# Where the first operands of a fused conv and quantized FFN are issued: ScalarE's queue or SyncE's

## The chip, the core and the metric

The kernel runs on one core of a Trainium2 chip. The metric is the device time of one execution in microseconds; below 291.45 us is the median of three executions. Lower is better.

## What is computed

`x` is 128 x 32 x 512 (tokens x channels x length), f32. A grouped 1-d convolution over the length (4 groups of 8 channels, 9 taps) is shifted by a conditional term, and the result goes through a feed-forward block whose activations and weights are all rounded to 8-bit steps; `x` is added at the end:

```python
out = conv(x, weight, groups=4, padding=4)            # 128 x 32 x 512
out = out + (c @ c_weight.T)[:, :, None] + bias[None, :, None]
gate = qlinear(out, w_gate)                           # 512 -> 1376
up   = qlinear(out, w_up)                             # 512 -> 1376
y = x + qlinear(silu(gate) * up, w_down)              # 1376 -> 512
# qlinear(x, w): x and w rounded by fake_quant to steps of max|row| / 127, then multiplied
```

## The kernel before

The convolution is done on TensorE: `x_windows` holds the input cut in 32 **spans** (4 groups g of 8 spans i, each 320 KB, 64 positions of 8 channels), and `toeplitz_cut[:, g]` holds the taps of group g spread as a **band** (80 KB for one group). `conv_span(q)` makes five windows of span q, each one f32 product that TensorE runs as two passes, so ten matmuls a span. It waits for the span (`span_in[q]`) and, at the first span of a group, for that group's band (`taps_in` for group 0). The small operands, `small_sb` (96 KB: the condition, its weight and the bias), give the per-channel shift: `multiply_ctx` on TensorE waits for `small_in`, `make_shift` on VectorE waits for it too, and every `add_shift` waits for `shift_ready`.

The weights `w_gate_up` come in 11 tiles of 512 KB (`load_w(j)`), the down weights in 4 pieces of 688 KB (`load_w_down(o)`). VectorE takes their row maxima (`weights_top`, `down_top`), GpSimd rounds them (`round_w`), TensorE turns them (`turn_gate_up`), ScalarE copies them out. Once the weights are in place, 32 channels run as tiles i = 0 to 31: gate and up products in three pieces (`gate_or_up`), silu, scaling, a maximum over the row, rounding, a DMA transpose, and the down product (`down`).

Each engine runs a fixed list of steps, written out by hand for the first part and as a loop from tile 7 on; nothing is moved at run time. What orders the start:

- **SyncE's queue** issues nearly all DMAs. It begins with `load_span(0)`, `load_span(1)`, `load_w(0)`, `load_span(2)`, `load_span(3)`, `load_span(4)`, `load_w(1)` and goes on alternating spans and weights. Its first wait is in `load_w(10)`, for the turn of weight tile 0 (`w_turned`, L311), and `load_w_down(0)` to `(2)` follow behind that.
- **ScalarE's queue** issues two DMAs at its start (L609, L610): the band of group 0 and the small operands. Then ScalarE waits for the small operands and runs one `Silu` on a column of them (L612, L613, the "silu trial", whose result nothing reads, so that the table of the activation is loaded early). Then come `copy_span(2)` and the rest.
- **VectorE** clears `warm_in` (L916, counted by `warm_ready`), then `weights_top(0)`, `make_shift`, `add_shift(0)`, `add_shift(1)`, `fold_y(1)`.
- **TensorE** waits for `warm_ready`, runs seven matmuls on the cleared tile (`run_empty(7)`), waits for the identity matrices, and goes through `conv_span(0)`, `conv_span(1)`, `multiply_ctx()`, `conv_span(2)` to `conv_span(8)`, `turn_gate_up(0)`, `conv_span(9)`, `conv_span(10)` and the turns of the weights.

Of the kernel before, what the change touches and what calls it, by code (L numbers as in the profile page):

```python
# [6 lines left out]
ACT = mybir.ActivationFunctionType  # L7
# [20 lines left out]
def adaln_ffn(nc, x, x_windows, cond_ctx_bias, taps_cut, w_gate_up, w_down, out):  # L28
    N, C, L = x.shape
    BLOCK = 4 * PAD  # L30
    CI = P // BLOCK
# [19 lines left out]
    CUT_WIDTH = LEAST + 2 * SHARED  # L51
# [16 lines left out]
    with ExitStack() as ctx:  # L68
        def sb(name, shape, dt=F32):
            return ctx.enter_context(nc.sbuf_tensor(name, shape, dt))  # L70

        def sem(name):
            return ctx.enter_context(nc.semaphore(name))
# [15 lines left out]
        toeplitz_cut = sb("toeplitz_cut", [P, GROUPS, CI, CUT_WIDTH])  # L89
        ident = sb("ident", [P, P])  # L90
        ident_bf = sb("ident_bf", [P, P], BF16)
        small_sb = sb("small_sb", [P, N + 2 * C])
        silu_trial = sb("silu_trial", [P, 1])
        warm_in = sb("warm_in", [P, P], BF16)
# [18 lines left out]
        def span_windows(g, i):  # L113
            return slabs[g % 2][:, WINDOWS * i:WINDOWS * (i + 1), :]
# [63 lines left out]
        small_in = sem("small_in")  # L178
        taps_in = sem("taps_in")
# [5 lines left out]
        warm_ready = sem("warm_ready")  # L185
# [104 lines left out]
        def rows(j):  # L290
            return P if j < JT - 1 else TAIL
# [4 lines left out]
        def _(sp):  # L296
            def load_span(q):
                g, i = divmod(q, SPANS)
                if i == 0 and g == 2:

                    sp.wait_ge(wdq_ready, KT - 1)
                elif i == 0 and g == 3:

                    sp.wait_ge(conv_done, 2 * SPANS)
                sp.dma_start(span_windows(g, i).rearrange("p w n -> p (w n)"), x_windows[g, :, i, :])\
                    .then_inc(span_in[q], 16)

            def load_w(j):
                if j >= W_SLOTS:

                    sp.wait_ge(w_turned, j - W_SLOTS + 1)  # L311
                r = rows(j)
                sp.dma_start(w_in[j % W_SLOTS][0:r, :, :], w_gate_up[P * j:P * j + r, :, :])\
                    .then_inc(w_tile_in[j % W_SLOTS], 16)
# [68 lines left out]
            def load_other_taps():  # L383
                sp.dma_start(toeplitz_cut[:, 2:, :, :].rearrange("p g c o -> p (g c o)"), taps_cut[:, 2 * CI * CUT_WIDTH:])\
                    .then_inc(taps_cut_in, 16)

            load_span(0)
            load_span(1)
            load_w(0)
            load_span(2)  # L390
            load_span(3)
# [214 lines left out]

        @block.scalar
        def _(act):
            act.dma_start(toeplitz_cut[:, 0, :, :].rearrange("p c o -> p (c o)"), taps_cut[:, 0:CI * CUT_WIDTH]).then_inc(taps_in, 16)  # L609
            act.dma_start(small_sb[:, :], cond_ctx_bias).then_inc(small_in, 16)  # L610

            act.wait_ge(small_in, 16)  # L612
            act.activation(silu_trial[:, :], small_sb[:, 0:1], ACT.Silu)  # L613

            def copy_span(q):
                g, i = divmod(q, SPANS)
# [776 lines left out]
```

## Time and profile before

| | us |
|---|---|
| median of three executions | 291.45 |
| fastest of the three / slowest of the three | 290.97 / 757.24 |
| the profiled execution, its own time | 292.09 |
| its span, first to last instruction | 290.3 |
| outside the span | 1.8 |
| TensorE busy / VectorE busy in the span | 279.6 / 250.0 |
| TensorE's granted clock over the span | 1.00 |

In the rows further down, PE is TensorE, PEld its weight loads, DVE VectorE, ACT ScalarE, POOL GpSimd, SPq and ACTq the issuing of SyncE and ScalarE; L305 is line 305 of the kernel. A DMA row tells how long the issue held the queue, and "to landing" is the time from the start of the issue to the completion that a waiting engine sees. Buffer numbers and tile shares of one memory are left out in names: `hq_mem<-w_gate_up` is one of the first six weight tiles, `slab<-x_windows` a span, `slab<-w_down` one of the first three down pieces.

### The profile page before, as it was taken

Reading aid. Unit: us, or ns where it says so; the run is one execution under the profiler, and the core shown is the slowest. Engines: PE = TensorE matmul, PEld = TensorE weight load, DVE = VectorE, ACT = ScalarE, POOL = GpSimd, SP = SyncE. Lnnn points to the kernel's source line nnn. Section 1 sums busy time; section 2 is a strip of 40 time slices with the busy share of each in tenths; the row PEclk is TensorE's granted clock in tenths of the full one; section 3 lists DMA queues with packets and bytes.
Section 4 is the critical chain, followed back from the end, with each engine's and each line's share of the span. In section 5 each row is a group of like instructions: output and inputs, shape, how many; then the busy total and the mean of one; then the engine's idle time right before and its main releaser. Section 6 shows DMA issues by size and latency. Waiting matters only on the chain.

```text
span 290.3 us, 4758 instructions
## 1 busy us (share of the span) xinstructions
PE 279.6 (96%) x1582; PEld 160.0 (55%) x1582; DVE 250.0 (86%) x410; ACT 193.8 (67%) x232; POOL 200.9 (69%) x209
## 2 busy tenths in 40 slices
PE   7897989999999999999999999999989999999995
PEld 4896656656455555554444656664434444444443
DVE  0998999899998998979888888898978889888885
ACT  2349989898687776555877744555688767666640
POOL 1469988999858786555788834556488887666623
PEclk9999999999999999999999999999999999999999
DMA  7999943594929999853599995523266683333346
GB/s 254 412 416 345 395 150 76 133 223 94 264 80 233 242 218 223 176 163 99 129 232 275 294 216 166 161 78 96 75 158 159 169 198 87 87 88 86 97 99 209
DMA packets 83848, 53.37 MB, mean 184 GB/s; under 512 B 69904, under 2 KB 70672, under 8 KB 83696
## 3 DMA queue, kind: packets, MB, share of 16 engines
q1 hardware_dynamic: 83536, 52.89, 66.8%
q8 instruction: 13, 0.21, 0.3%
q10 hardware_dynamic: 288, 0.18, 0.2%
q14 instruction: 11, 0.09, 0.1%
HBM read 27.75 MB, written 8.39 MB: 125 GB/s over the span
## 4 chain that ended last, share of the span: by engine, by line
PE 78%; DMA 8%; DVE 5%; POOL 4%; issue 3%; SPq 0%; ACT 0%; DVEq 0%; POOLq 0%
PE bank L1201 45%; PE bank L1221 20%; PE bank L1103 12%; DMA slab<-w_down 6%; DMA slab<-x_windows 2%; POOL sg_mem L519 2%; DVE h_mem L879 1%; DVE h_max L884 1%; DVE sg_mem L866 1%; POOL slab L527 1%; DVE hq_mem L905 1%; POOL xo_mem L527 0%; POOL yq_mem L500 0%; DVE y_part L844 0%; POOL y_mem L510 0%
## 5 line engine op out<-in xcount | busy, mean ns | idle before, releaser
L1201 PE MATMUL bank<-wgu_t,xq_mem 128*128 128x512 bf16 (+1 forms) x768 | 155.8, 357 | 2.6 <-DVE sg_mem L866 1.3
L519 POOL TENSOR_TENSOR sg_mem<-sg_mem,gu_scale_row 128x512 f32<-128x512 f32 (+1 forms) x96 | 111.2, 1165 | 60.7 <-ACT sg_mem L665 60.6
L1201 PEld LDWEIGHTS bank<-wgu_t,xq_mem 128*128 128x128 bf16 x768 | 73.8, 98 | 74.2 <-DVE h_mem L879 7.9
L665 ACT ACTIVATE sg_mem<-sg_mem,x_scale 128x512 f32<-128x512 f32 (+1 forms) x96 | 62.7, 672 | 38.9 <-DVE sg_mem L866 38.7
L1221 PE MATMUL bank<-wd_t,hq_mem 128*128 128x512 bf16 (+1 forms) x341 | 78.6, 379 | 0.1
L879 DVE SCALAR_TENSOR_TENSOR h_mem<-bank,x_scale,sg_mem 128x512 f32<-128x512 f32 (+1 forms) x96 | 65.8, 690 | 11.1 <-POOL sg_mem L519 9.2
L866 DVE TENSOR_TENSOR sg_mem<-bank,gu_scale_row 128x512 f32<-128x512 f32 (+1 forms) x96 | 59.8, 626 | 13.7 <-PE bank L1201 13.6
L670 ACT ACTIVATE h_mem<-h_mem,h_inv 128x1376 f32<-128x1376 f32 (+1 forms) x32 | 45.1, 1414 | 25.5 <-DVE h_inv L786 25.5
L1221 PEld LDWEIGHTS bank<-wd_t,hq_mem 128*128 128x128 bf16 (+1 forms) x341 | 33.3, 98 | 40.4 <-DMA hq_mem<-hq_mem 0.6
L884 DVE TENSOR_REDUCE h_max<-h_mem 128x1 f32<-128x1376 f32 x32 | 50.3, 1575 | 0.0
L1103 PEld LDWEIGHTS bank<-toeplitz_cut,slab 128*128 128x128 f32 x320 | 43.0, 191 | 4.5 <-issue 1.3
L1103 PE MATMUL bank<-toeplitz_cut,slab 128*128 128x160 f32 (+1 forms) x320 | 43.8, 290 | 1.4 <-DMA slab<-x_windows 0.8
L678 ACT ACTIVATE hq_mem<-h_mem 128x1376 bf16<-128x1376 f32 (+1 forms) x32 | 41.8, 1310 | 0.1
L527 POOL TENSOR_TENSOR xo_mem<-xo_mem,hq_mem 128x512 f32<-128x512 f32 x24 | 30.5, 1273 | 1.9 <-DMA xo_mem<-x 1.9
L905 DVE SCALAR_TENSOR_TENSOR hq_mem<-bank,h_scale,wd_scale_row 128x512 f32<-128x512 f32 x31 | 23.0, 743 | 1.5 <-POOL slab L527 1.3
L629 ACT ACTIVATE y_mem<-y_mem,x_inv 128x512 f32<-128x512 f32 x24 | 16.1, 710 | 2.1 <-DVE x_inv L786 2.1
L500 POOL TENSOR_SCALAR yq_mem<-y_mem 128x512 bf16<-128x512 f32 x22 | 13.3, 619 | 3.0 <-ACT y_mem L629 3.0
L844 DVE TENSOR_REDUCE y_part<-y_mem 128x8 f32<-128x1024 f32 x12 | 14.6, 1214 | 0.2
L793 DVE TENSOR_REDUCE gu_max<-hq_mem 128x2 f32<-128x1024 f32 (+1 forms) x7 | 8.3, 1198 | 6.6 <-DMA hq_mem<-w_gate_up 6.6
L510 POOL TENSOR_TENSOR y_mem<-y_mem,shift 128x512 f32<-128x512 f32 x7 | 7.3, 1050 | 9.3 <-ACT y_mem L622 9.3
L483 POOL TENSOR_SCALAR hq_mem<-hq_mem,gu_inv 128x512 f32<-128x512 f32 (+1 forms) x14 | 9.5, 693 | 3.2 <-DVE gu_inv L805 3.2
L641 ACT ACTIVATE wgu_t<-bank 128x1024 bf16<-128x1024 int16 (+1 forms) x11 | 10.9, 1034 | 0.4 <-PE bank L1119 0.4
(63 smaller groups left out, 136.4 us busy)
## 6 DMA issues: line engine op xcount, KB each, us to landing
slab<-x_windows SPq DMA_DIRECT2D x32, 320.0 KB, 4.1
xo_mem<-x SPq DMA_DIRECT2D x24, 256.0 KB, 2.9
out<-xo_mem SPq DMA_DIRECT2D x24, 256.0 KB, 2.2
hq_mem<-w_gate_up SPq DMA_DIRECT2D x6, 512.0 KB, 8.9
slab<-w_down SPq DMA_DIRECT2D x3, 688.0 KB, 15.0
h_mem<-w_gate_up SPq DMA_DIRECT2D x4, 512.0 KB, 13.5
slab<-x SPq DMA_DIRECT2D x1, 2048.0 KB, 9.7
out<-slab SPq DMA_DIRECT2D x7, 256.0 KB, 2.0
```

The costliest lines, as they stand in the source:

```text
L519: pool.tensor_tensor(s, s, gu_scale_row[:, 1, at:at + n], ALU.mult).then_inc(silu_scaled, 1)
L527: pool.tensor_tensor(xo_of(i), xo_of(i), down_out[:, i % 2, :], ALU.add).then_inc(out_ready, 1)
L665: act.activation(s, s, ACT.Silu, scale=x_scale[:, i:i + 1]).then_inc(silu_done, 1)
L670: act.activation(hi, hi, ACT.Copy, bias=MAGIC, scale=h_inv[:, i:i + 1]).then_inc(h_rounded, 1)
L678: act.activation(hq[i % HQ_BUFS][:, first:INTER], h[i % H_BUFS][:, first:], ACT.Copy, bias=-MAGIC)\
L866: dve.tensor_tensor(sg[i % SG_BUFS][:, at:at + n], gate_bank[(NP * i + p) % 2][:, 0:n], gu_scale_row[:, 0, at:at + n], ALU.mult).then_inc( ...
L879: dve.scalar_tensor_tensor(h[i % H_BUFS][:, at:at + n], up_bank[(NP * i + p) % 2][:, 0:n], x_scale[:, i:i + 1], sg[i % SG_BUFS][:, at:at + ...
L884: dve.tensor_reduce(h_max[:, i:i + 1], h[i % H_BUFS], AX_X, ALU.max, apply_absolute_value=True)\
L905: dve.scalar_tensor_tensor(down_out[:, i % 2, :], down_bank_of(i)[:, :], h_scale[:, i:i + 1], wd_scale_row[:, :], ALU.mult, ALU.mult).then ...
L1103: last = pe.matmul(out_span[:, :, lo:hi], span_windows(g, i)[:, k, :], toeplitz_cut[:, g, :, tap:tap + hi - lo], start=(k == 0), stop=(k = ...
L1201: last = pe.matmul(bank[n % 2][:, 0:cols], xq_t[:, g, k, P * c:P * (c + 1)], wgu_t[:, m, k, at:at + cols], start=(k == 0), stop=(k == KT - 1))
L1221: last = pe.matmul(down_bank_of(i)[:, :], hq_t[i % HQT_BUFS][0:r, j, :], wd_t[0:r, j, :], start=(j == 0), stop=(j == JT - 1))
```

## The change

The two DMAs of ScalarE's queue go to SyncE's: the band of group 0 becomes its very first DMA, ahead of span 0, and the small operands its fourth, behind span 1 and ahead of weight tile 0. The silu trial no longer waits for the small operands and reads them; it waits for the cleared tile `warm_in` and reads a column of that. Nothing else differs: the same bytes are moved, and every consumer waits on the same semaphores.

```diff
@@ SyncE
+            sp.dma_start(toeplitz_cut[:, 0, :, :].rearrange("p c o -> p (c o)"), taps_cut[:, 0:CI * CUT_WIDTH]).then_inc(taps_in, 16)
             load_span(0)
             load_span(1)
+            sp.dma_start(small_sb[:, :], cond_ctx_bias).then_inc(small_in, 16)
             load_w(0)
             load_span(2)
             load_span(3)
@@ ScalarE
-            act.dma_start(toeplitz_cut[:, 0, :, :].rearrange("p c o -> p (c o)"), taps_cut[:, 0:CI * CUT_WIDTH]).then_inc(taps_in, 16)
-            act.dma_start(small_sb[:, :], cond_ctx_bias).then_inc(small_in, 16)
-
-            act.wait_ge(small_in, 16)
-            act.activation(silu_trial[:, :], small_sb[:, 0:1], ACT.Silu)
+
+            act.wait_ge(warm_ready, 1)
+            act.activation(silu_trial[:, :], warm_in[:, 0:1], ACT.Silu)
```

## Rows read from the trace of the kernel before

**Rows 1.** Busy time by stretch: us, PE, PEld, DVE, ACT, POOL, clock, DMA share, GB/s.

```profile
0.00:10.00 10.00, 7.58 (x42) 5.38 (x43) 2.58 (x5) 1.61 (x3) 1.21 (x10) 1.00 0.82 297
...
40.00:280.00 240.00, 238.78 (x1263) 128.73 (x1262) 212.91 (x353) 169.51 (x197) 172.13 (x165) 1.00 0.64 158
```

**Rows 2.** Waits of TensorE, whole span: line, waited for, us in total, times, longest.

```profile
PE bank L1119 <- POOL hq_mem L483: 1.5, 3, 0.7
PE bank L1201 <- DVE sg_mem L866: 1.3, 1, 1.3
PE bank L1103 <- DMA slab<-x_windows: 0.8, 1, 0.8
PE bank L1103 <- DMA toeplitz_cut<-taps_cut: 0.6, 1, 0.6
```

**Rows 3.** The chain that ended last, in order of time, first 39 us: start, us.

```profile
1.66 0.42 SPq L313
2.08 0.04 issue
2.12 6.16 DMA slab<-x_windows
8.28 0.04 issue
8.33 9.29 PE bank L1103 x70
...
20.74 16.16 DMA slab<-w_down
```

**Rows 4.** Timeline of TensorE, 0 to 17 us: start, us, instruction, idle before.

```profile
4.60 2.75 PE L1103 MATMUL bank<-toeplitz_cut,slab 128*128 128x112 f32 x20 [0.61 <-DMA toeplitz_cut<-taps_cut]
7.19 0.32 PE L1175 MATMUL bank<-small_sb 128*128 128x32 f32 x2
8.33 9.29 PE L1103 MATMUL bank<-toeplitz_cut,slab 128*128 128x112 f32 x70 [0.82 <-DMA slab<-x_windows]
```

**Rows 5.** One issue a query: taps, then small operands, span 0, weight tile 0.

```profile
L609 ACTq DMA_DIRECT2D toeplitz_cut<-taps_cut x1: 407/407/407, 0.7 to 0.7; - x1
DMA to landing us min/median/max: 3.7/3.7/3.7
...
DMA to landing us min/median/max: 4.2/4.2/4.2
...
DMA to landing us min/median/max: 3.5/3.5/3.5
...
DMA to landing us min/median/max: 5.8/5.8/5.8
```

**Rows 6.** Timeline of SyncE's queue, 0 to 21 us.

```profile
0.74 0.87 SPq L305 DMA_DIRECT2D slab<-x_windows  x2
...
12.64 1.43 SPq L313 DMA_DIRECT2D h_mem<-w_gate_up  x2
18.09 0.34 SPq L313 DMA_DIRECT2D hq_mem<-w_gate_up  x1
```

**Rows 7.** Busy time from the start to six moments; last column GB/s over it.

```profile
0.00:2.00 2.00, 1.01 (x3) 0.43 (x4) 0.11 (x1) 0.33 (x1) 1.21 (x10) 1.00 0.15 22
0.00:2.50 2.50, 1.51 (x4) 0.58 (x5) 0.11 (x1) 0.83 (x1) 1.21 (x10) 1.00 0.27 45
0.00:3.50 3.50, 2.51 (x6) 0.89 (x7) 0.11 (x1) 1.28 (x1) 1.21 (x10) 1.00 0.46 121
0.00:4.50 4.50, 3.00 (x7) 0.89 (x7) 0.11 (x1) 1.28 (x1) 1.21 (x10) 1.00 0.58 178
0.00:6.00 6.00, 4.40 (x18) 2.31 (x19) 0.11 (x1) 1.49 (x2) 1.21 (x10) 1.00 0.68 226
3.00:37.00 34.00, 30.32 (x269) 26.15 (x268) 27.58 (x42) 20.50 (x30) 21.80 (x29) 1.00 1.02 385
```

**Rows 8.** Timeline of ScalarE, 0 to 10 us.

```profile
1.67 1.28 ACT L613 ACT_TABLE_LOAD   x1 [1.67 <-PEq L1387]
5.45 0.20 ACT L613 ACTIVATE silu_trial<-small_sb 128x1 f32<-128x1 f32 x1 [2.50 <-DMA small_sb<-cond_ctx_bias]
9.88 0.60 ACT L622 ACTIVATE y_mem<-bank 128x512 f32<-128x512 f32 x1 [4.22 <-PE bank L1103]
```

**Rows 9.** Timeline of VectorE, 7 to 38 us.

```profile
7.50 1.22 DVE L793 TENSOR_REDUCE gu_max<-hq_mem 128x2 f32<-128x1024 f32 x1 [6.57 <-DMA hq_mem<-w_gate_up]
8.63 0.18 DVE L821 TENSOR_TENSOR shift<-bank,small_sb 128x32 f32<-128x32 f32 x1
...
36.92 1.58 DVE L809 TENSOR_REDUCE d_max<-slab 128x1 f32<-128x1376 f32 x1 [0.37 <-DMA slab<-w_down]
```

## Prediction

> **What bounds the kernel now.** I read the busy time by stretches first. From 40 to 280 us TensorE works for 238.78 of 240 us at a granted clock of 1.00 [rows 1]; nothing that is issued in the first 15 us can shorten that, so the change can only be worth what it alters at the start. There TensorE is busy 7.58 of the first 10 us [rows 1], and the table of its waits says what for: 0.6 us for the band of group 0 and 0.8 us for a span near the beginning, then 1.5 us behind GpSimd's rounding and 1.3 us behind VectorE later [rows 2]. The 0.6 us is the wait that the change aims at. Whether it counts is told by the timeline: the first two spans run from 4.60 to about 7.3, the small product to 7.51, and then TensorE idles 0.82 us more, until span 2 has landed [rows 4]. So two waits stand in a row, and the second ends last. An earlier start of the first span only makes the second wait longer, as long as span 2 lands where it does now. The chain of waits agrees: it doesn't pass through the band, it passes through the landing of span 2 at 8.28, 70 matmuls, and then the landing of the third down piece at 36.90 [rows 3].
>
> The third thing to read is what those landings hang on. From 3 to 37 us the DMA engines are busy at a share of 1.02, moving 385 GB/s [rows 7]. Span 2 is issued at 2.12 and lands 6.16 us later, the down piece 16.16 us after its chain step [rows 3], while span 0 needed 3.5 us [rows 5]: these transfers stand in line behind the bytes ahead of them. In this stretch the time is set by the sum of bytes, and only where the line runs dry by the moment of issue.
>
> **The change, part by part.**
>
> *The small waits on ScalarE.* Removed: two issues on ScalarE's queue, of 0.41 us for the band, and the wait of the trial. The table load starts at 1.67, behind the issues, and the trial runs at 5.45 after 2.50 us of waiting; then ScalarE idles 4.22 us until the first span that it copies [rows 8]. After, the table load can start near 0.8 and the trial near 2.1. That is worth 0: the next work of ScalarE waits for TensorE, not for the trial. The cover is those 4.22 us, and the new wait is for a memset of VectorE that TensorE's warm-up waits for as well. If that cover were gone, the trial would cost its 0.20 us.
>
> *The band goes first on SyncE.* It saves nothing in bytes and delays span 0 by one issue. Two issues hold the queue for 0.87 us in all [rows 6], so one step is some 0.45 us. Now the band lands at 0.74 + 3.7 = 4.5 and span 0 at 0.74 + 3.5 = 4.2, and the first matmul starts at 4.60 [rows 4, 5]. After, the start hangs on span 0. Lower bound: the two shared the engines, and their sum of bytes is served by the same moment as now, so span 0 lands at about 4.2, and TensorE starts 0.3 us earlier. Upper bound: the landing moves by the whole step, 4.2 + 0.45 = 4.7, and TensorE starts at 4.75, 0.15 us later than now. Even then the first two spans and the small product, 2.9 us as they run now (4.60 to 7.51 [rows 4]), end at 7.66, ahead of 8.28. Worth to the end: 0 on both bounds, with 0.6 us of cover.
>
> *The small operands behind span 1.* Issued at about 2.1 rather than 1.18. They landed 4.2 us after their issue, at 5.4 [rows 5]. A shift of the full 0.9 us gives 6.3; the small product is not reached before 7.1, and the shift is made at 8.63, behind the maximum of weight tile 0 [rows 4, 9]. Cost 0, cover 0.8 us.
>
> *What is queued behind them.* Every later DMA of SyncE is issued later, weight tile 0 and span 2 by two steps, 0.9 us. This is the only part that can reach the end, so it is worked through with bytes. From the start of the first issue (0.74) to the first data is about 1 us: 44 KB have moved by 2.0 [rows 7]. In units of 1000 bytes the new line is: band 82, span 0 328, span 1 328, small 98, weight tile 0 524, then span 2. What was moved by a moment is the mean rate by the length: 112 by 2.5, 424 by 3.5, 801 by 4.5, 1356 by 6.0 [rows 7]. So the engines reach the bytes of
>
> - span 0 (82 ahead) at 2.2; it is available at 1.19 + 1.0 = 2.2: just in time
> - span 1 (410 ahead) at 3.5; available at 2.6
> - small operands (738 ahead) at 4.3; available at 3.1
> - weight tile 0 (836 ahead) at 4.6; available at 3.5
> - span 2 (1360 ahead) at 6.0; available at 4.0
>
> Only at span 0 can the line run dry, and by no more than one step, 0.45 us. Behind it the margin is 0.9 us and grows. Later, SyncE ends its run of issues at 14.07 and stands until 18.09 for the turn of weight tile 0 [rows 6]; 0.9 us more of issuing falls into those 4.0 us. If that cover were gone, the remaining weight tile and the down pieces would be issued up to 0.9 us later, and they stand in line for over 12 us anyway.
>
> So the shift of the DMA stream, call it d, has bounds of nothing lost and 0.45 us lost, and below nothing too: the order by which two queues shared the engines in the first 5 us is gone, and the third down piece is waited for by VectorE with 0.37 us of idle time [rows 9], so at most 0.37 us could be gained before VectorE's own work ends last. I take d = +0.1: the arithmetic says that the line is just supplied, and the packets that meet the slow first microsecond are now the band's small ones, so a few bytes less get through in it. From the down piece d goes on to the end in full, since VectorE's next steps release TensorE (the 1.3 us wait [rows 2]) and TensorE has no slack after 40 us.
>
> The Trainium skill ("DMA: Bandwidth & Descriptors", section "Issuing engines are not separate DMA queues") says that all issuing engines use the same 16 DMA engines, and that issuing from several only saves the sequencer's issue time. That speaks against this change, since it gives up exactly that saving: by the rule alone, with the issue time taken as it stands, the sum would be two steps worse, which is the first rival below; by the rows the saving is hidden behind the line.
>
> **Sum.** Start of the first span -0.3 to +0.15, worth 0; trial 0; small operands 0; stream +0.1 (-0.37 to +0.45). The profiled execution, 290.3 in its span and 1.8 around it, becomes 290.4 and 292.2. That execution stands 0.6 us above the median of the runs, so against the median of 291.45 the forecast is 291.55; I give 291.5.
>
> **Rivals.**
>
> *A, slower: the issue time goes through.* The chain runs over the issues ahead of span 2 (L313 ends at 2.08, span 2 is issued at 2.12 [rows 3]). If landings follow the issue and not the line, weight tile 0 and span 2 come 0.9 us later: span 2 at 9.2, VectorE's first maximum at 8.4 instead of 7.50 [rows 9], and everything that was DMA-bound or VectorE-bound moves with them: 291.45 + 0.9 = 292.35. It decides from the point where d exceeds 0. For it: the chain as printed. Against it: 6.16 us from issue to landing where 3.5 is possible, and a share of 1.02. A chance of 0.13.
>
> *B, faster: the start is gained.* The band no longer trickles in between the packets of spans 0 and 1, the stream starts with small packets in the slow first microsecond and runs at its full rate sooner, and span 2, weight tile 0 and the down piece all land earlier. Price: up to the 0.37 us of VectorE's idle time before the third down piece: 291.45 - 0.37 = 291.1. It decides if span 2 lands before 8.1. Against it: the bytes are the same. A chance of 0.20.
>
> *C, the fixed order falls into another step.* A shift of some tenths lets the loop meet another wait, such as the one of 1.1 us on VectorE that the busy shares show as 238.78 of 240 [rows 1]. All waits of TensorE named in rows 2 sum to 4.2 us, so doubling one of them costs some 1.5 us (292.95), losing one gains as much (289.95). A chance of 0.07.
>
> The forecast itself holds 0.60. Its own range is the spread of executions, which for the kernel before goes from 290.97 to 292.09, shifted by 0.1. The range down to B's gain and up to A's cost on the same spread is 290.97 - 0.37 = 290.6, and 292.09 + 0.9 = 293.0; I give 290.5 to 292.9.
>
> Two per cent, about what a measurement of this kernel can tell from no change, is 5.8 us. No case comes near: A and B stay within it, and C would need several waits at once. I leave 0.01 for faster and 0.02 for slower, 0.97 for within.
>
> **What would show it.** Right, if in the changed kernel TensorE's first span starts between 4.2 and 4.8, waits for `slab<-x_windows` and no longer for the band, if span 2 still lands at 8.2 to 8.5 with TensorE's second wait as long as the first start allows, if weight tile 0 is seen by VectorE at 7.4 to 7.7, if the third down piece lands at 36.7 to 37.2, and if the trial runs near 2.1 with ScalarE's next copy still near 9.9. If span 2 lands at 9.2, A holds; if the DMA stream ends before 36.6, B. The forecast is wrong if the stream's share between 2 and 3 us drops by more than 0.45 us of work, or if an engine past 40 us shows a wait that isn't there now.

## The result and the profile after

The changed kernel is slower: a median of 293.64 us against 291.80 us for the kernel before, 16 executions of each. The ratio of the fast executions, which leaves out the one of 757.24 us, is 1.0054 with a 95% interval of 1.0034 to 1.0074, so 1.6 us, from 1.0 to 2.2. That is within the 2% of the forecast's main case, but outside its range of 290.5 to 292.9. The profiled execution took 293.72 us with a span of 291.9, against 292.09 and 290.3.

The chain of waits of the changed kernel, in order of time, from the fourth issue on (start, us, what):

```profile
2.11 0.43 SPq L390
2.54 0.04 issue
2.59 0.43 SPq L313
3.02 0.04 issue
3.06 5.96 DMA slab<-x_windows
9.03 0.04 issue
9.07 9.32 PE bank L1103 x70
...
21.50 16.00 DMA slab<-w_down
```

Against [rows 3], span 2 is issued at 3.06 rather than 2.12, and it lands at 9.02 rather than 8.28. The two added issues moved it by 0.94, and 0.74 of that arrived. The third down piece lands at 37.50 rather than 36.90. The chain still doesn't pass through the band.

TensorE's timeline and ScalarE's, of the changed kernel:

```profile
4.59 3.92 PE L1103 MATMUL bank<-toeplitz_cut,slab 128*128 128x112 f32 x20 [0.43 <-issue]
8.35 0.32 PE L1175 MATMUL bank<-small_sb 128*128 128x32 f32 x2
...
2.02 0.20 ACT L613 ACTIVATE silu_trial<-warm_in 128x1 f32<-128x1 bf16 x1
10.62 0.60 ACT L622 ACTIVATE y_mem<-bank 128x512 f32<-128x512 f32 x1 [8.39 <-PE bank L1103]
```

The first span starts at 4.59, as before (4.60 [rows 4]); nothing was gained there even locally. But the 20 matmuls of the first two spans now take 3.92 us, until 8.5, rather than 2.75. That isn't the change's doing, and it is no wait: a matmul takes some 480 ns up to 6.5 us, where it takes some 290 ns in the kernel before, and the granted clock stands at 1.00 in both. The kernel before has it too, in a second profile of the unchanged text (taken further down), first TensorE's timeline and then the chain of waits:

```profile
4.71 5.22 PE L1103 MATMUL bank<-toeplitz_cut,slab 128*128 128x112 f32 x20 [0.55 <-DMA toeplitz_cut<-taps_cut]
...
0.73 3.84 DMA toeplitz_cut<-taps_cut
4.57 0.14 issue
4.71 5.22 PE bank L1103 x20
```

Over the twenty profiles the same 20 matmuls take from 2.75 to 5.22 us; why isn't shown. The trial runs at 2.02 without a wait and gives nothing, since ScalarE's next copy waits for TensorE until 10.62; it stood at 9.88 [rows 8].

Where the DMA engines lost the time is told by the busy time from 4 to 8 us (us, PE, PEld, DVE, ACT, POOL, clock, DMA share, GB/s). Before, and then after:

```profile
4.00:8.00 4.00, 2.90 (x22) 2.82 (x22) 0.50 (x1) 0.20 (x1) 0.00 (x0) 1.00 1.01 389
```

```profile
4.00:8.00 4.00, 3.57 (x18) 3.44 (x18) 0.00 (x0) 0.00 (x0) 0.00 (x0) 1.00 0.90 306
```

83 GB/s less over 4 us are 332 KB, which take 0.85 us at the 389 GB/s of the kernel before. This stretch, in which the forecast had the engines well supplied, holds most of what the start lost.

Where the start's loss has arrived at TensorE is best read at its first eight gate and up products in one run, just behind the down pieces (before, then after):

```profile
39.16 1.90 PE L1201 MATMUL bank<-wgu_t,xq_mem 128*128 128x512 bf16 x8 [1.34 <-DVE sg_mem L866]
```

```profile
39.77 1.90 PE L1201 MATMUL bank<-wgu_t,xq_mem 128*128 128x512 bf16 x8 [1.00 <-DVE sg_mem L866]
```

They are 0.61 us later. In the profiles of all experiments this row starts at 38.47 to 39.50 us in the eight that issue their DMAs up to 7 us as the kernel before does, and at 39.59 to 40.09 in the five that do it as the changed one does; the means are 0.7 us apart.

The other place is at 81 us, at GpSimd's first residual add (before, then after):

```profile
81.00 2.52 POOL L527 TENSOR_TENSOR xo_mem<-xo_mem,hq_mem 128x512 f32<-128x512 f32 x2 [1.92 <-DMA xo_mem<-x]
```

```profile
82.33 2.50 POOL L529 TENSOR_TENSOR xo_mem<-xo_mem,hq_mem 128x512 f32<-128x512 f32 x2 [2.64 <-DMA xo_mem<-x]
```

GpSimd was free for it at 81.00 - 1.92 = 79.08 and at 82.33 - 2.64 = 79.69: the start's 0.61 us. Then it waited 0.72 us longer for residual 0, and from there to the end both stay in the distance (1.3 us, and 0.3 more at the end, where the changed kernel's TensorE waits 0.5 us for a turn). In sixteen of the eighteen profiles that issue residual 0 in its place, the span is the start of this add and 209.2 to 209.8 us; so what two profiles differ by is nearly all made ahead of it. So one profile has two parts, and the experiments take them in turn.

### The profile page after: what moved, and what is told of

It reads as the page before. It is cut to its first block, busy times and chain, and to the rows that moved or that the text cites. A ratio compares the mean times of both kernels' runs of the same rounds, so it can differ in the third digit from the quotient of the medians.

```text
span 291.9 us, 4758 instructions
## 1 busy us (share of the span) xinstructions
PE 281.1 (96%) x1582; PEld 161.2 (55%) x1582; DVE 249.4 (85%) x410; ACT 193.8 (66%) x232; POOL 200.8 (69%) x209
## 4 chain that ended last, share of the span: by engine, by line
PE 70%; DMA 11%; DVE 5%; issue 4%; POOL 4%; ACT 3%; SPq 2%; DVEq 0%; POOLq 0%; ACTq 0%
PE bank L1201 41%; PE bank L1221 17%; PE bank L1103 11%; DMA slab<-w_down 5%; POOL sg_mem L521 2%; DMA slab<-x_windows 2%; DMA xo_mem<-x 2%; ACT h_mem L670 1%; DMA hq_mem<-hq_mem 1%; DVE h_mem L879 1%; DVE h_max L884 1%; ACT hq_mem L678 1%; POOL xo_mem L529 1%; DVE sg_mem L866 1%; POOL yq_mem L502 1%
## 5 line engine op out<-in xcount | busy, mean ns | idle before, releaser
L1103 PEld LDWEIGHTS bank<-toeplitz_cut,slab 128*128 128x128 f32 x320 | 44.2, 195 | 4.8 <-DMA slab<-x_windows 1.4
L1103 PE MATMUL bank<-toeplitz_cut,slab 128*128 128x160 f32 (+1 forms) x320 | 45.0, 295 | 1.3 <-DMA slab<-x_windows 0.9
L622 ACT ACTIVATE y_mem<-bank 128x512 f32<-128x512 f32 x7 | 4.2, 594 | 11.8 <-PE bank L1103 11.8
```

Source lines behind the costliest of these rows:

```text
L1103: last = pe.matmul(out_span[:, :, lo:hi], span_windows(g, i)[:, k, :], toeplitz_cut[:, g, :, tap:tap + hi - lo], start=(k == 0), stop=(k = ...
```

## Experiments

Theory I: what counts is the issue step, a DMA put ahead of weight tile 0 and span 2 on SyncE's queue. Rivals: S, the sharing of the engines by two queues; the trial; and G, later C, for the second part.

| kernel | median us | before beside it | ratio, 95% |
|---|---|---|---|
| band alone | 292.87 | 292.19 | 1.0016, 0.9995 to 1.0037 |
| small operands alone | 293.00 | 292.19 | 1.0027, 1.0010 to 1.0045 |
| trial alone | 292.28 | 292.19 | 0.9998, 0.9982 to 1.0014 |
| the change again | 293.90 | 292.19 | 1.0062, 1.0040 to 1.0084 |
| two useless DMAs, early | 293.56 | 291.70 | 1.0061, 1.0039 to 1.0082 |
| weight tile 0 by ScalarE | 291.73 | 291.70 | 1.0003, 0.9981 to 1.0025 |
| residual 0 earlier, before | 292.04 | 291.70 | 1.0010, 0.9996 to 1.0025 |
| residual 0 earlier, changed | 293.63 | 291.70 | 1.0055, 1.0033 to 1.0077 |
| four useless DMAs, early | 293.82 | 291.89 | 1.0076, 1.0042 to 1.0109 |
| two useless DMAs, at 7 us | 292.99 | 291.89 | 1.0034, 1.0012 to 1.0057 |
| span 1 by ScalarE | 292.44 | 291.89 | 1.0019, 1.0001 to 1.0037 |
| spans 3 and 4 in one DMA | 293.09 | 291.89 | 1.0038, 1.0016 to 1.0061 |
| ten small matmuls, before | 292.41 | 292.53 | 0.9998, 0.9979 to 1.0017 |
| ten small matmuls, changed | 293.28 | 292.53 | 1.0023, 1.0005 to 1.0041 |
| six warm-ups fewer | 294.87 | 292.53 | 1.0073, 1.0042 to 1.0103 |
| thirty small matmuls | 292.65 | 292.23 | 1.0007, 0.9987 to 1.0026 |

### The parts of the change, one by one

```diff
 # band alone: SyncE
+            sp.dma_start(toeplitz_cut[:, 0, ...], taps_cut[:, 0:CI * CUT_WIDTH]).then_inc(taps_in, 16)
             load_span(0)
             load_span(1)
 # small operands alone: SyncE
+            sp.dma_start(small_sb[:, :], cond_ctx_bias).then_inc(small_in, 16)
             load_w(0)
 # trial alone: ScalarE
+            act.wait_ge(warm_ready, 1)
+            act.activation(silu_trial[:, :], warm_in[:, 0:1], ACT.Silu)
```

> Only the band of group 0 goes to SyncE's queue, first; the small operands and the trial stay as before. Theory I (issue steps: each DMA put ahead of weight tile 0 and span 2 on SyncE's queue moves their landings by nearly its 0.45 us, and so the end): span 2 lands near 8.65, half of the change's loss, +0.6 to +0.9 us. Theory S (sharing: what is lost is the sharing of the engines by two queues in the first microseconds, since the band alone leaves the engines empty from 2.5 to 3 us): nearly the whole loss, +1.3 to +1.6 us, with the DMA share of 2.5 to 3.0 us at about 0.6 as in the changed kernel.

> Only the small operands go to SyncE's queue, behind span 1; the band stays first on ScalarE's. Theory I (issue steps): weight tile 0 and span 2 one step later, span 2 at 8.65, +0.6 to +0.9 us. Theory S (sharing in the first microseconds): nothing is empty between 2.5 and 3 us, span 2 stays near 8.3, 0 to +0.2 us.

> Only the silu trial's wait and input are changed; both DMAs stay on ScalarE's queue. Theories I and S: no difference (-0.2 to +0.2 us), the table load still starts at 1.67 behind the two issues. A theory that the trial matters would have +0.5 us or more.

> The changed kernel once more, as the measure for the three others on the same chip: +1.3 to +1.9 us, and a second profile of it. Theory I: span 2 lands at 9.0 again. If the landing of span 2 differs by 0.5 us or more between the two profiles while the time doesn't, the start isn't what the loss hangs on.

Measured: +0.7 for the band (its interval reaches just below nothing), +0.8 for the small operands, +0.1 for the trial, and +1.7 for all. The parts add up within their intervals, and both issues are near the half that theory I gave them. The trial is out. S had expected next to nothing of the small operands, 0 to +0.2; their interval, from 0.3 us on, excludes that. It had also expected a DMA share of 0.6 from 2.5 to 3.0 us with the band alone; that was 1.08. Nor did span 2 land at 8.65: with the band alone it landed at 9.08, and with the small operands alone TensorE began it at 8.45. From 4 to 8 us the engines moved 295 GB/s with the band alone and 350 with the small operands alone:

```profile
4.00:8.00 4.00, 3.73 (x23) 3.60 (x22) 0.00 (x0) 0.00 (x0) 0.00 (x0) 1.00 0.90 295
```

```profile
4.00:8.00 4.00, 2.93 (x23) 2.82 (x22) 0.33 (x1) 0.20 (x1) 0.00 (x0) 1.00 0.95 350
```

### Issue steps without bytes

```diff
+            sp.dma_start(tiny[:, 0:2], cond_ctx_bias[:, 0:2]).then_inc(tiny_in, 16)
             load_span(0)
             load_span(1)
+            sp.dma_start(tiny[:, 2:4], cond_ctx_bias[:, 2:4]).then_inc(tiny_in, 16)
             load_w(0)
```

> The kernel before, with both operands still on ScalarE's queue, and two DMAs of 8 bytes a partition added to SyncE's at the two places where the change puts its own (ahead of span 0, behind span 1). They are work of no use; the output is as before. Theory I (issue steps: weight tile 0 and span 2 land later because they are issued two steps later): nearly the full loss of the change, +1.2 to +1.8 us, VectorE's first maximum at 8.0 or later. Theory S (the loss is that the band and the small operands leave ScalarE's queue, so that one queue alone must keep the engines busy): 0 to +0.3 us, the maximum at 7.5.

Measured: +1.9 us, the whole loss, with ScalarE's queue as it was and 1 KB in each added DMA. VectorE's first maximum and the stretch from 4 to 8 us of this kernel:

```profile
8.78 1.22 DVE L798 TENSOR_REDUCE gu_max<-hq_mem 128x2 f32<-128x1024 f32 x1 [7.85 <-DMA hq_mem<-w_gate_up]
...
4.00:8.00 4.00, 3.16 (x14) 3.04 (x13) 0.00 (x0) 0.20 (x1) 0.00 (x0) 1.00 0.85 294
```

The maximum comes at 8.78, where it was 7.50 [rows 9], and the rate is lower than the changed kernel's 306. S falls; it is the steps on SyncE's queue.

Do twice as many cost twice as much, and does it matter where they stand?

```diff
 # four: two ahead of span 0, two behind span 1
 # late: one ahead of and one behind load_taps_of_group_1()
             load_span(8)
+            sp.dma_start(tiny[:, 0:2], cond_ctx_bias[:, 0:2]).then_inc(tiny_in, 16)
             load_taps_of_group_1()
+            sp.dma_start(tiny[:, 2:4], cond_ctx_bias[:, 2:4]).then_inc(tiny_in, 16)
             load_w(3)
```

> The kernel before with four useless DMAs of 8 bytes a partition on SyncE's queue, two ahead of span 0 and two behind span 1. Theory I (each early issue step costs): two steps cost 1.9 us, so four cost 3.4 to 4.2 us, and the engines move some 220 GB/s or less between 4 and 8 us (389 before, 294 with two). A theory that the loss comes from the first step that uncovers the engines and then saturates: 1.7 to 2.4 us.

> The kernel before with the two useless DMAs placed later on SyncE's queue, around the load of the band of group 1 at 7.2 us. Theory L (only steps issued before the line of transfers has built up count, since later ones lie behind 8 us of queued bytes): 0 to +0.3 us. A theory that every issue on SyncE's queue costs, because the queue itself is the bound all the way: +1.5 us or more.

Both missed. Four steps cost +1.9 in the median, with an interval of 1.2 to 3.2 us: that excludes the 3.4 and more of theory I, but not that four cost more than two. In their profiles they do, with the eight products at 41.05 against 40.43; from 4 to 8 us the engines moved 323 GB/s. Late steps leave the start as it is in the profile (394 GB/s from 4 to 8 us, the eight products at 39.15), and yet the median is +1.1 with an interval from 0.4 to 1.7. So two added DMAs can cost as much as that without touching the start, and a part of what the early ones cost need not be made there either. Something differs between executions that a single profile doesn't catch.

### Fewer steps than before

```diff
 # weight tile 0 by ScalarE's queue, behind the small operands
-            load_w(0)
+            act.dma_start(w_in[0][0:P, :, :], w_gate_up[0:P, :, :]).then_inc(w_tile_in[0], 16)
 # span 1 by ScalarE's queue, between the band and the small operands
-            load_span(1)
+            act.dma_start(span_windows(0, 1)..., x_windows[0, :, 1, :]).then_inc(span_in[1], 16)
 # spans 3 and 4 in one DMA; conv_span(3) waits for span_in[4]
-            load_span(3)
-            load_span(4)
+            sp.dma_start(slabs[0][:, WINDOWS * 3:WINDOWS * 5, :]..., x_windows[0, :, 3:5, :]...).then_inc(span_in[4], 16)
```

> The opposite of the change: weight tile 0 goes from SyncE's queue to ScalarE's, behind the small operands, so that span 2 and all later DMAs of SyncE are issued one step earlier. Theory I: span 2 lands at 7.9 rather than 8.3 and the end moves by -0.3 to -0.8 us. Theory S or a stream bound by its bytes alone: 0 within 0.2 us. A rival: tile 0 shares the engines with spans 2 to 4 and VectorE's first maximum comes later than 7.5, then +0.2 to +0.6 us.

> Span 1 goes from SyncE's queue to ScalarE's, between the band and the small operands, so that weight tile 0, span 2 and all later DMAs of SyncE are issued one step earlier and weight tile 0 isn't held back on a shared queue. Theory I with steps that still cost in the kernel before: -0.3 to -0.8 us. If the kernel before is already supplied from 4 to 8 us (389 GB/s of the 415 that the engines reach later), nothing is left to gain: -0.2 to +0.2 us.

> Spans 3 and 4 of the kernel before are loaded by one DMA of 640 KB, so that weight tile 1 and everything behind it are issued one step earlier; the price is that span 3 is only seen when span 4 has landed too, at about 9.9 rather than 9.1, and TensorE reaches span 3 at 9.6. Theory I (steps cost): the gain of a step, up to -0.4, against 0.3 us of waiting for span 4, so -0.1 to +0.3. If steps behind span 2 don't count: +0.2 to +0.4.

None gained. With tile 0 on ScalarE's queue span 2 was issued at 1.68 but landed at 9.10, not at the 7.9 of theory I, and tile 0 itself reached VectorE at 8.93; yet the rate is 394 GB/s and the median that of the kernel before. So a late span 2 alone doesn't cost; the versions that lose at the start are those with a lower rate from 4 to 8 us. With span 1 on that queue, +0.5. The merged load is the instructive one. Its start is the best of all:

```profile
4.00:8.00 4.00, 3.62 (x26) 3.49 (x26) 1.36 (x2) 0.20 (x1) 0.00 (x0) 1.00 1.05 421
```

and its first residual add is

```profile
81.98 2.49 POOL L527 TENSOR_TENSOR xo_mem<-xo_mem,hq_mem 128x512 f32<-128x512 f32 x2 [3.91 <-DMA xo_mem<-x]
```

GpSimd was free at 78.07, 1.0 us ahead of the kernel before, and waited 3.91 us in place of 1.92. In this profile the gain of the start was given back twice over, and the median was +1.2.

### Is it the gate at 81 us?

```diff
             turn_hq(3)
+            load_residual(0)
             load_span(18)
             load_span(19)
-            load_residual(0)
```

> The kernel before, with the load of residual 0 issued ahead of spans 18 and 19 rather than behind them (near 76 us). In the profiles GpSimd's first residual add waits for it at 81 us and everything behind it moves by what it is late. Theory G (the gate at 81 us takes a part of the change's loss): here it is worth 0 to -0.8 us, as the gate is sometimes closed in this kernel too. A theory in which all of the loss is made in the first 40 us: 0 within 0.2.

> The changed kernel with the same move of residual 0. Theory G: of the loss of 1.7 us against the kernel before, only the part made in the first 40 us is left, 0.6 to 1.0 us, and the step at 81 us is gone from the profile. A theory in which all of the loss is made in the first 40 us: still +1.5 to +1.9 us.

Theory G gets no support: with residual 0 issued ahead of the two spans the medians are still 1.6 us apart, and neither is faster. It isn't excluded, since the two ratios differ by 0.0045 with an uncertainty of 0.0026, so by 0.5 to 2.1 us, and G had 0.6 to 1.0. In the profile of the kernel before the first add then came at 78.89, but the second waited 2.38 us for VectorE:

```profile
78.89 1.27 POOL L527 TENSOR_TENSOR xo_mem<-xo_mem,hq_mem 128x512 f32<-128x512 f32 x1 [0.29 <-DMA xo_mem<-x]
82.53 1.27 POOL L527 TENSOR_TENSOR xo_mem<-xo_mem,hq_mem 128x512 f32<-128x512 f32 x1 [2.38 <-DVE hq_mem L905]
```

The place is a gate, but opening it alone only hands the wait on.

### What holds the residual up: a load of the instruction queue

In the profile with the merged load, residuals 1 and 2, issued at about 72 us, take 6 us to land, and the turn behind them 6.9; in the kernel before it is 3.3 and 4.2. Between them a packet of 16 KB stands on the queue called "instruction" (q8). There are 13 of them in the page for 1582 matmuls, one to 122. Theory C: that load, falling among the transposes and residuals, is slow and holds them up. The unchanged kernel was profiled a second time for it:

> The kernel before once more, as it is, for a second profile of it: all theories have the third down piece at 36.4 to 37.0 us and 388 to 396 GB/s between 4 and 8 us. Theory C: if the load on the instruction queue stands ahead of 72 us and takes about 1 us there is no step at 81 us, and if it takes over 2 us there is one of 1.4 to 2.0 us.

Its span was 292.0 and its time 293.79, with nothing changed. The DMA queues in the microsecond of the load, first of the profile that the prediction rests on (70 to 71 us), then of this one (74 to 75 us):

```profile
q8 instruction: 1, 0.02, 6.0%
```

```profile
q8 instruction: 1, 0.02, 15.7%
```

6.0% of 16 engines for 1 us is 0.96 us for the one packet, and 15.7% is 2.5 us. And this profile's issues of the two residuals, its queue and its add:

```profile
L341 SPq DMA_DIRECT2D xo_mem<-x x2: 413/468/524, 72.9 to 73.5; - x2
DMA to landing us min/median/max: 5.6/5.6/5.7
...
73.95 3.41 SPq L352 DMA_TRANSPOSE hq_mem<-hq_mem  x1
77.41 1.05 SPq L305 DMA_DIRECT2D slab<-x_windows  x2
78.56 0.38 SPq L341 DMA_DIRECT2D xo_mem<-x  x1
...
82.83 2.49 POOL L527 TENSOR_TENSOR xo_mem<-xo_mem,hq_mem 128x512 f32<-128x512 f32 x2 [3.52 <-DMA xo_mem<-x]
```

The turn's issue holds the queue 3.41 us (2.28 before), residual 0 is issued 1.4 us later, and the add waits 3.52, 1.6 us more, as theory C had it for a load of over 2 us. All profiles with residual 0 in its place, by their load (its share times 16 us) and the add's wait:

| load near 64 to 79 us | profiles | wait of the add, us |
|---|---|---|
| 64 to 72 us, 1.0 to 1.5 us long | before; trial; change again; change, third profile; two early; two late; ten matmuls, changed; six fewer; thirty | 1.92; 1.57; 1.95; 1.86; 1.57; 1.62; 1.52; 1.76; 1.12 |
| 77 to 79 us, 1.0 to 1.2 us long | change; small operands; tile 0 by ScalarE | 2.64; 2.95; 2.51 |
| 73 to 76 us, 1.9 to 3.1 us long | before, second profile; band; span 1 by ScalarE; merged; four early; ten matmuls, before | 3.52; 3.33; 3.74; 3.91; 3.90; 2.94 |

The first group stands apart from the other two (at most 1.95 against at least 2.51); the second and the third touch (2.95 and 2.94). The same kernel stands in the first and the third (the kernel before), and in the first and the second (the changed one). So the wait goes with when the load falls, and that isn't fixed by the kernel's text. Which of the two sets the other is open. In ten profiles the load ahead of this one stands at 44 to 49 us and the one behind it at 94 to 96 (85 with the thirty matmuls below), but this one between 64 and 78, and at 69, 70 and 78 in the three of the changed kernel: it may be late and long because the transfers around it are, and not the other way round. That was tried by moving the load:

```diff
 # ten, in the kernel before and in the changed one
             run_empty(7)
+            for _ in range(10):
+                pe.matmul(conv_bank(3)[:, 0:32], warm_in[:, :], warm_in[:, 0:32], start=True, stop=True)
 # six warm-ups fewer
-            run_empty(7)
+            run_empty(1)
 # thirty: run_empty(4) and the loop over range(30)
```

> The kernel before with ten more matmuls of 32 columns on the cleared tile behind run_empty (work of no use, in time in which TensorE waits for the band anyway), so that TensorE's program is 20 instructions longer ahead of everything. Theory C (a 16 KB load on the instruction queue, one to about 125 of TensorE's matmuls, falls near 70 to 78 us; where it falls among the DMA transposes and residual loads issued at 71 to 75 us it takes 2.5 us rather than 1.0, holds them up and costs 1.4 to 2.0 us at GpSimd's first residual add): the load comes 2 us earlier, clear of them, -0.2 to -0.8 us in the median and no step at 81 us in the profile. Rival R (the step at 81 us has nothing to do with that load): 0 within 0.2 us, steps as often as before.

> The changed kernel with the same ten matmuls. Theory C: no step at 81 us either, so that against the same edit of the kernel before only the part made in the first 40 us is left, +0.7 to +1.1 us. Rival R: still +1.6 to +1.9 us apart.

> The kernel before with run_empty(1) in place of run_empty(7): TensorE's program is 12 instructions shorter ahead of everything (six warm-up matmuls are left out, their result is not used). Theory C: the load on the instruction queue comes about 1.3 us later, at 71 to 73 us, among the transposes and residual loads more often: +0.5 to +1.5 us, with a load of over 2 us and a step of 1.4 to 2.0 us at 81 us in the profile. Rival R: 0 within 0.2 us, unless TensorE's granted clock falls, which the profile would show.

In the kernel before, the ten matmuls did not clear the place: the load stands at 73 us with 1.9 us, within the 70 and 74 of that kernel's own two profiles, the add waits 2.94, and the median doesn't move. In the changed kernel the load went to 68 us, the add waits only 1.52, and the medians of the two are 0.87 us apart, as theory C had it. The two ratios (0.9998 and 1.0023) differ by 0.0025 with an uncertainty about as large, so this doesn't separate 0.9 from 1.6 us for certain.

Six warm-ups fewer missed its place (70 us): no step at 81 us, but another one. (The first two spans take 5.22 us there, no more than in the second profile of the kernel before, and GpSimd is free at 79.44, so the missing warm-ups didn't cost at the start.) The last turn, in the chain of waits of that kernel:

```profile
281.43 4.96 DMA hq_mem<-hq_mem
286.39 0.05 issue
286.44 4.26 PE bank L1337 x22
```

TensorE waits 2.2 us for it, and a load stands in this stretch at 283 us (9.1% of 1 us, 1.5 us), where the kernel before has it at 278.7, ahead of its last turn. The median is +2.3 us. A load near a turn and a late turn again stand together. Right behind the wait the granted clock falls, and from 287 to 290 us it is 0.50, the lower of its two levels. The 22 matmuls there take 4.24 us, where the kernel before takes 2.58, and that is 1.7 us of the loss on top of the wait:

```profile
287.00:290.00 3.00, 3.00 (x16) 2.14 (x15) 0.91 (x2) 0.00 (x0) 0.00 (x0) 0.50 0.46 175
```

> The kernel before with run_empty(4) and thirty matmuls of 32 columns in place of run_empty(7): TensorE's program is 54 instructions longer ahead of everything, its first 4.5 us take as long as now. Theory C (code load among the transposes): all loads of the instruction queue come some 5 us earlier, the one of 70 to 78 us at 65 to 70 us, where only transposes with slack stand, and the one at 279 us well ahead of the last transpose: no step at 81 us and -0.3 to -0.8 us in the median, so that it beats the kernel before. If the moment of the load is not set by TensorE's program, or the step is rare in the timed runs: 0 within 0.2 us.

> The changed kernel once more, for a third profile: 300 to 310 GB/s between 4 and 8 us and the third down piece 0.6 to 0.9 us later than in the kernel before. Theory C: a step of over 1.4 us at 81 us only if the load on the instruction queue takes over 2 us there.

The thirty matmuls moved the load to 65 us and there is no step (a wait of 1.12), but GpSimd came free for the add at 80.01, 0.93 us later than in the kernel before, and nothing is gained: +0.4 with an interval on both sides of nothing, where theory C had -0.3 to -0.8. What the step is worth in the medians isn't shown. No version beat the kernel before. The third profile of the changed kernel fits: 309 GB/s from 4 to 8 us, GpSimd free at 79.51, load at 70 us, a wait of 1.86 and a span of 290.9.

## Why the prediction was wrong

**What bounds the kernel** was right in its first half: the 0.6 us for the band was no gain. That span 2 ends last belongs to the one profile it was read from. In the second profile of the same kernel the chain runs over the band, the first two spans (5.22 us) and VectorE, TensorE begins span 2 only at 10.04, and its eight products still start at 39.39, 0.23 us later than in the first. And with weight tile 0 on ScalarE's queue span 2 landed at 9.10 at no cost. What carried the loss is the DMA stream as a whole, as the prediction says one paragraph further on.

**The trial, the band and the small operands** as consumers: right. 0 for the trial is measured (0.9998), TensorE's first span starts at 4.59 within the forecast 4.2 to 4.75, and the small operands are in time.

**What is queued behind them** is the step that failed. The sum took the transfers as one line that the 16 engines serve at the mean rate, and supposed that a DMA is there to be served 1.0 us after its issue; it found only span 0 short, a margin of 0.9 us and more behind it, and took d = +0.1. Measured at the down piece, d was 0.60, and over the four profiles with the changed start and residual 0 in its place GpSimd stood free at 79.5 to 80.4 ahead of the first add, against 79.08 and 79.31 in the two of the kernel before. Its premise that a line with bytes left keeps the engines busy is refuted by the share of 0.90 and the 306 GB/s between 4 and 8 us, in which by the sum 0.9 us and more stood in reserve. The amounts moved by each moment, against which the new line was set, had been read from a kernel that had issued five DMAs by 2.1 us, two of them on ScalarE's queue, where the changed one has issued three. It moved less from there on: 357 KB rather than 424 by 3.5 us, 1122 rather than 1356 by 6.0 us and 1752 rather than 2160 by 8.0. The issue time "goes through", as rival A said: span 2 at 9.0 (A: 9.2), the first maximum at 8.24 (A: 8.4), and 0.7 us on average at the eight products (A: 0.9). The 6.16 us from issue to landing were read as waiting in line and so as cover; 0.94 us later in issue was 0.74 later in landing. What was held against A, that a long queue covers the issues, had been argued from the length of the queue and not bounded by any row.

The rule of the Trainium skill named in the prediction ("DMA: Bandwidth & Descriptors", section "Issuing engines are not separate DMA queues") was the better guide: what the change gives up is the issue time. Its remark that this time "is usually small relative to the DMA itself" doesn't hold here: a step of 0.45 us stands beside a span of 328 KB, 0.84 us at 389 GB/s.

**Sum and range.** The upper bound of the stream, 0.45 us, counted only the step ahead of span 0, though weight tile 0 and span 2 move by two, since it let a loss be made only where the line is short by bytes. Even A with its 0.9 us gives only 292.35. Of what is left, 0.35 us isn't the change's: the kernel before has a median of 291.80 in the runs of the result, not 291.45. The remaining 0.9 us or so were in no forecast but C, "the fixed order falls into another step", priced at 1.5 us and given 0.07. Such a step is what the profiles show at 81 us, but as something that comes and goes in the same kernel.

**Open.** Shown is that two DMAs added on SyncE's queue, ahead of span 0 and of weight tile 0, cost what the change costs, whatever they carry, and that some 0.7 us of it are lost by the eight products at 39 us. Why the engines run at a share of 0.90 with issued bytes outstanding isn't shown. The second part, from there to the 1.6 us of the result, isn't settled. The load at 73 to 76 us stands beside every wait of more than 3 us in eighteen profiles, but that it is the cause isn't shown, and none of the three profiles of the changed kernel is in that group. The late steps' +1.1 us with an untouched start is unexplained by all of it.

## What to carry to other kernels

At the start of a kernel, count the issues ahead of the transfer that the chain passes through, and allow for their time going through in full, until an experiment with nearly empty DMAs in their place says otherwise (here two steps of 0.45 us took 0.7 us at the start and 1.6 to 1.9 us in the medians); here the idle engine's queue was the better place for the small operands. A long time from issue to landing is not proof of cover: read the busy share of the DMA engines and the GB/s in the stretch, and expect both to drop when the issues slip. For differences under 1%, take more than one profile of the kernel before: here two of the same text differ by 1.7 us in their span, 1.6 of it at one gate.

## What the runs showed of the hardware

- Two DMAs of 1 KB on SyncE's queue, one ahead of span 0 and one behind span 1, lowered the rate of the 320 to 512 KB transfers from 389 to 294 GB/s between 4 and 8 us, and the busy share of the DMA engines from 1.01 to 0.85. Four left it at 323 GB/s.
- A 16 KB packet of the instruction queue took 1.0 to 1.5 us in twelve profiles and 1.9 to 3.1 us in the six in which it fell at 73 to 76 us, behind a DMA transpose. In those six the residual loads took 5.0 to 6.0 us to land in the median rather than 3.3 to 4.0, and in five of them the issue of the next turn held SyncE's queue 3.0 to 3.9 us rather than 1.3 to 2.3.
- The first 20 f32 matmuls took from 2.75 to 5.22 us in kernels whose granted clock stands at 1.00 there, and both ends in two profiles of one kernel.
- Behind 2.2 us of standing still near the end, TensorE's granted clock was 0.50 from 287 to 290 us, and 22 matmuls took 4.24 us rather than 2.58.
- Ten matmuls of 32 columns in idle time cost nothing that can be measured (0.9998, 0.9979 to 1.0017).
